# The 64 steps of a decoder's mixer phase: the same work dealt anew over five kinds of body

## What is computed

```python
x = x + mamba(layernorm(x))
x = x + cross_attention(layernorm(x), ctx, mask)       # one head of 256, softmax over 1601
x = x + routed_ffn(layernorm(x))                       # top 2 of 8 experts, width 704

def mamba(x):                                          # 512 inner channels, 16 states
    xs, res = split(x @ W_in.T)
    xs = silu(causal_conv4(xs) + b_conv)
    B = (xs @ W_x.T)[:, :16]
    dt = softplus(xs @ W_dt.T + b_dt)
    # per channel c and state n, along the tokens t:
    h[t] = exp(dt[t] * A[c, n]) * h[t - 1] + dt[t] * B[t, n] * xs[t]
    y[t] = sum_n h[t] + D[c] * xs[t]
    return (y * silu(res)) @ W_out.T
```

## Time and profile before

| what | us |
|---|---|
| median of 3 runs | 1064.59 (1064.29 to 1067.52) |
| profiled execution, span | 1119.2 |
| FIRST, from its first scan to that of the next body | 116.10 |
| STEADY, first of two | 155.30 |
| LAST | 145.00 |
| DRAIN, up to 720 us | 93.80 |

### The profile page before, as it was taken

One profiled execution on the slowest core, in us unless ns is written; L12 is line 12 of the kernel. 1 busy time (PEld: TensorE's weight loads), 2 busy tenths in 40 slices (PEclk: granted clock), 3 DMA queues, 4 the chain that ended last, 5 costly groups with the idle time before them and its releaser, 6 DMA issues. The chain is left out here.

```text
span 1119.2 us, 16281 instructions
## 1 busy us (share of the span) xinstructions
PE 908.4 (81%) x5148; PEld 723.8 (65%) x5149; DVE 670.0 (60%) x1091; ACT 446.0 (40%) x827; POOL 599.3 (54%) x499
## 2 busy tenths in 40 slices
PE   5767667899969999788998779736279999999665
PEld 2344345576856677665677647735279999999564
DVE  5188789887789877876878433275034444443215
...
GB/s 321 157 199 1 2 113 38 1 15 1 40 264 1 16 1 2 199 103 7 9 1 110 42 7 8 20 155 191 146 39 115 115 115 75 78 37 70 61 89 90
DMA packets 48955, 85.45 MB, mean 76 GB/s; under 512 B 6292, under 2 KB 38696, under 8 KB 46856
## 3 DMA queue, kind: packets, MB, share of 16 engines
...
## 5 line engine op out<-in xcount | busy, mean ns | idle before, releaser
L413 POOL TENSOR_TENSOR u<-dtx,b_all 128x512 f32<-128x512 f32 x256 | 324.9, 1281 | 176.6 <-DVE h L662 172.9
L662 DVE TENSOR_TENSOR_SCAN h<-da,u 128x512 f32<-128x512 f32 x256 | 307.5, 1215 | 55.8 <-ACT da L497 33.9
L497 ACT ACTIVATE da<-dt_,a_neg 128x512 f32<-128x512 f32 x256 | 174.5, 690 | 105.9 <-DVE h L662 105.2
L785 PEld LDWEIGHTS ysum<-ident,h 128*128 128x128 f32 x1024 | 128.4, 152 | 94.5 <-DVE h L662 45.0
L785 PE MATMUL ysum<-ident,h 128*128 128x128 f32 x1024 | 157.7, 293 | 32.5 <-DVE h L662 25.5
L1421 DVE TENSOR_TENSOR hid<-act_,ps_u 128x352 f32<-128x352 f32 x78 | 40.4, 521 | 134.7 <-ACT act_ L1272 128.4
L965 PE MATMUL pv<-pT,ctx_n 128*128 128x128 f32 (+1 forms) x832 | 104.6, 276 | 1.4 <-DVE x_all L722 1.3
L965 PEld LDWEIGHTS pv<-pT,ctx_n 128*128 128x128 f32 (+1 forms) x832 | 98.4, 192 | 6.5 <-DVE x_all L722 3.2
L936 PE MATMUL pa<-ctx_t,xnT_a 128*128 128x401 f32 (+1 forms) x256 | 94.2, 502 | 3.6 <-ACT xnT_a L548 1.8
L1272 ACT ACTIVATE act_<-ps_g 128x352 f32<-128x352 f32 x78 | 36.1, 465 | 149.9 <-PE ps_u L1535 92.6
L1559 PE MATMUL ps_y<-w_hi,hidT_hi 128*128 x234 | 68.1, 291 | 19.0 <-issue 15.0
...
## 6 DMA issues: line engine op xcount, KB each, us to landing
...
```

The source lines that it names most:

```text
L413: nc.gpsimd.tensor_tensor(u[:, i % 2, :], dtx[:, j % 2, :], b_all[:, n, :], ALU.mult).then_inc(u_ok, 1)
L497: nc.scalar.activation(da[i % DS][:], dt_[:, j % 2, :], ACT.Exp, scale=a_neg[:, j, n:n + 1]).then_inc(da_ok, 1)
L662: nc.vector.tensor_tensor_scan(h[:, i % HS, :], da[i % DS][:], u[:, i % 2, :], 0.0, ALU.mult, ALU.add).then_inc(scan_ok, 1)
L785: last = nc.tensor.matmul(ysum[:, t * P:(t + 1) * P], h[:, i % HS, t * P:(t + 1) * P], ident[:], is_transpose=True, start=n == 0 and t == ...
```

## The change

All step numbers of the five tables are dealt anew. No instruction is added or removed, no tile, semaphore or line of the engines' programs changes, nor the order in which groups are added in PSUM. The order of SP's queue is the same in both, and so is every engine's order in FILL, although most of its numbers differ. The tables are four lines longer, so what was L662 is L666 in the kernel after. The diff, cut: of each table the lines that hold the numbers spoken of below.

```diff
 STEADY = {
-    "y_copy": 1, "y_turn": 2, "read_out": 3, "out_proj": (4, 4, 4, 4), "x1": (6, 7), "ln_a_stat": 7, "ln_a_root": 8,
-    "ln_a_norm": 8, "ln_a_turn": 8, "ln_a_copy": 10, "x_bias": 11, "query_const": 10, "query": (10, 10),
-    "row_const": 12, "query_copy": 12,
+    "y_copy": 1, "y_turn": 2, "read_out": 3, "out_proj": (4, 4, 4, 4), "x1": (7, 7), "ln_a_stat": 7, "ln_a_root": 7,
+    "ln_a_norm": 7, "ln_a_turn": 7, "ln_a_copy": 11, "x_bias": 20, "query_const": 10, "query": (10, 10),
+    "row_const": 11, "query_copy": 13,
...
-    "pick": ((14, 15, 16, 17), (17, 18, 19, 21), (26, 27, 28, 29), (34, 36, 38, 39)), "fill": (14, 14, 24, 35),
+    "pick": ((14, 15, 16, 17), (17, 18, 19, 21), (23, 27, 28, 29), (35, 36, 37, 38)), "fill": (15, 17, 24, 36),
...
-    "p_turn": ((20, 22, 22, 23), (29, 30, 30, 32), (38, 39, 39, 41), (46, 47, 47, 49)),
+    "p_turn": ((21, 22, 22, 23), (29, 30, 30, 31), (38, 39, 40, 40), (44, 47, 49, 51)),
...
-    "av_copy": (30, 41, 47, 54), "out": (31, 40, 47, 54), "x2": (32, 42, 47, 58), "ln_f_stat": 58, "ln_f_root": 60,
-    "ln_f_norm": 59, "ln_f_turn": 59, "ln_f_copy": 61, "router": (59, 60, 60, 60), "scores": 63, "ln_m_stat": 0,
+    "av_copy": (29, 42, 48, 56), "out": (31, 40, 48, 53), "x2": (32, 42, 49, 56), "ln_f_stat": 56, "ln_f_root": 58,
+    "ln_f_norm": 58, "ln_f_turn": 58, "ln_f_copy": 60, "router": (59, 59, 60, 60), "scores": 62, "ln_m_stat": 0,
...
-    "tap": (5, 10, 12, 14), "conv": (4, 10, 12, 14), "res_proj": ((19, 23), (24, 25), (28, 29), (30, 31)),
+    "tap": (6, 10, 13, 14), "conv": (6, 10, 12, 14), "res_proj": ((14, 16), (24, 25), (28, 28), (29, 30)),
...
 FIRST = {
     **STEADY,
-    "ln_m_norm": 0, "ln_m_turn": 0, "ln_m_copy": 2, "in_proj": ((3, 3), (6, 7), (7, 8), (8, 9)),
...
-    "dt_proj": ((50, 51, 52, 55), (3, 5, 5, 6), (13, 16, 17, 19), (32, 32, 33, 34)), "softplus": (57, 8, 23, 38),
-    "dt_add": (57, 10, 23, 38), "dtx": (60, 14, 28, 39),
+    "softplus": (57, 9, 23, 41), "dt_add": (57, 10, 23, 41), "dtx": (59, 14, 25, 43),
 }
 LAST = {
     **STEADY,
-    "out_proj": (4, 4, 5, 5), "x1": (5, 7), "ln_a_root": 7, "query_const": 9,
+    "read_out": 2, "x1": (5, 7), "ln_a_root": 9, "ln_a_norm": 8, "ln_a_turn": 9, "ln_a_copy": 10, "x_bias": 10,
+    "row_const": 10, "query_copy": 14,
...
-    "pick": ((13, 15, 16, 17), (17, 18, 19, 21), (26, 27, 28, 29), (34, 36, 38, 39)), "fill": (13, 14, 23, 35),
...
+    "pick": ((13, 15, 16, 17), (17, 18, 19, 21), (26, 27, 28, 29), (35, 37, 39, 40)), "fill": (12, 17, 24, 34),
...
+    "av_copy": (30, 41, 47, 55), "out": (30, 39, 47, 52), "x2": (31, 41, 47, 55), "ln_f_root": 57, "ln_f_norm": 57,
```

More of the change, by code:

```diff
@@ L85 @@
+    "tap": (6, 10, 13, 14), "conv": (6, 10, 12, 14), "res_proj": ((14, 16), (24, 25), (28, 28), (29, 30)),
+    "res_copy": (27, 27, 29, 34), "silu": 35, "b_proj": (34, 34, 39, 39), "b_copy": 43,
+    "dt_proj": ((48, 54, 55, 57), (4, 4, 6, 6), (14, 19, 21, 21), (33, 34, 34, 35)), "softplus": (60, 8, 24, 37),
+    "dt_add": (60, 9, 26, 39), "dtx": (62, 14, 28, 44),
 }
@@ L87 @@
     **STEADY,
[L88 to L91 removed]
+    "ln_m_stat": 4, "ln_m_norm": 11, "ln_m_turn": 2, "ln_m_copy": 2, "in_proj": ((2, 2), (7, 8), (9, 13), (13, 16)),
+    "tap": (2, 3, 5, 7), "conv": (12, 12, 16, 17), "res_proj": ((18, 20), (20, 21), (24, 25), (26, 26)),
+    "res_copy": (7, 7, 9, 12), "silu": 17, "b_proj": (31, 31, 31, 34), "b_copy": 18,
+    "dt_proj": ((35, 35, 38, 41), (), (), ()), "softplus": (24, 7, 10, 11), "dt_add": (28, 11, 23, 27),
+    "dtx": (30, 7, 20, 24), "a_exp": 18,
 }
@@ L114 @@
     **STEADY,
-    "out_proj": (3, 3, 4, 4), "ln_a_root": 6, "ln_a_norm": 7, "ln_a_turn": 9, "query_const": 9, "row_const": 13,
-    "query_copy": 11, "score": ((12, 13, 13, 14), (15, 15, 16, 17), (22, 22, 23, 26), (31, 32, 32, 34)),
-    "pick": ((13, 14, 15, 16), (16, 17, 18, 20), (24, 25, 26, 27), (32, 34, 36, 37)), "fill": (13, 13, 25, 34),
-    "max": (16, 20, 28, 42), "exp": (18, 25, 33, 45), "inverse": (21, 24, 34, 44),
-    "p_turn": ((20, 20, 21, 21), (27, 28, 28, 30), (37, 38, 40, 40), (45, 46, 48, 49)),
-    "p_copy": ((19, 20, 21, 23), (28, 29, 30, 32), (39, 41, 42, 43), (46, 47, 48, 49)),
-    "av": ((20, 20, 20, 22, 22, 23, 27), (30, 30, 30, 33, 33, 36, 37), (40, 40, 40, 41, 41, 42, 45), (48, 48, 49, 50, 51, 51, 52)),
-    "av_copy": (29, 39, 46, 52), "out": (30, 40, 46, 55), "x2": (32, 42, 46, 56), "ln_f_norm": 63, "ln_f_turn": 56,
-    "router": (57, 59, 60, 60),
+    "read_out": 0, "out_proj": (5, 5, 5, 8), "x1": (2, 4), "ln_a_stat": 6, "ln_a_root": 12, "ln_a_norm": 12,
+    "ln_a_turn": 9, "ln_a_copy": 16, "x_bias": 15, "row_const": 13, "query_copy": 18,
+    "score": ((14, 14, 14, 15), (16, 17, 17, 18), (21, 23, 23, 24), (30, 32, 33, 34)),
+    "pick": ((13, 14, 15, 16), (16, 17, 18, 19), (21, 23, 24, 28), (32, 33, 36, 38)), "fill": (2, 10, 32, 35),
+    "max": (17, 20, 30, 40), "exp": (18, 28, 35, 44), "inverse": (21, 21, 31, 52),
+    "p_turn": ((19, 19, 20, 21), (28, 28, 29, 30), (37, 37, 40, 40), (41, 46, 47, 49)),
+    "p_copy": ((22, 23, 27, 29), (32, 33, 34, 35), (42, 44, 46, 48), (49, 51, 54, 56)),
+    "av": ((20, 20, 22, 23, 23, 23, 27), (29, 29, 29, 31, 32, 35, 37), (40, 40, 40, 40, 42, 42, 44), (46, 46, 46, 48, 48, 49, 49)),
+    "av_copy": (32, 38, 48, 57), "out": (29, 38, 46, 54), "x2": (29, 45, 46, 53), "ln_f_stat": 53, "ln_f_root": 59,
+    "ln_f_norm": 60, "ln_f_turn": 54, "ln_f_copy": 63, "router": (54, 55, 60, 63), "scores": 60,
 }
```

37 lines of the change are left out of this document (16 added, 21 removed).

## The result

The kernel after takes **1033.88 us** (median of 4 runs, 1030.95 to 1035.07) beside 1064.44 (1063.35 to 1067.52) for the kernel before: a ratio of 0.9704, with a 95% interval of 0.9685 to 0.9722, or 30.6 us less. The forecast was 1049, with a range down to 1037: the direction was right and the gain nearly twice what was said.

The account below looks back on a forecast made before the run. Bounds differ by body: GpSimd's pace in FIRST, TensorE in STEADY and DRAIN, mixed in LAST. Terms -3.0 - 5.0 - 5.0 - 2.5 - 0.5 = -16.0, carried to the timed 1064.6 as 15.2 to 16: 1049 us, range 1037 to 1065.

Parts of the forecast that it names:

- The pause of step 23: STEADY: VectorE picks row tile 2 before its fill is done, waiting about 2.9 us; costed at nothing.
- The term of 1.2 at scan 40: FIRST: a scan's wait behind a dtx product goes as dtx falls into VectorE's pause; 1.2 of 3.7 us saved.
- (a) to (c): STEADY: earlier attention LayerNorm, later first convolution, query copy and fills moved; VectorE 2.4 us earlier, nothing counted on PE.
- the two new blocks: STEADY: out-projection 3 may wait for attT, row tile 3's first turn for its exponential; +1.4 us for both.
- The gap that I priced at -2.4: STEADY: PE's 4.85 us wait before the final LayerNorm's turn shrinks to about 2.4, by earlier statistics and normalisation.
- the seam: LAST into DRAIN: earlier final LayerNorm lets PE's queue drain about two scans sooner; -2.5 us, PE's gap near 4.
- (a) read_out: LAST: last read_out from step 3 to 2, so out_proj can begin earlier; -1.5 us.
- (b) the root: LAST: attention's root on ScalarE moves behind da(8), step 7 to 9, removing the scan's 1.09 us wait; -1.1 us.
- (c) the query copy: LAST: copy from step 12 to 14, two more scans run during the 4.62 us wait; half counted, -1.2 us.
- (d) read_out 1 ahead of the pick: LAST: read_out 1 precedes row tile 3's first pick, inside VectorE's 5.03 us wait; -1.2 us.
- rival 2: Whole kernel: the whole gain comes through, VectorE's gains are kept; -26, so 1039 us; chance 0.13.
- Rival 3: STEADY and LAST: PE stands before work whose ScalarE and GpSimd steps are later; slower, +5, so 1070 us; chance 0.10.

Follow-up runs that it names:

- the tail alone: Kernel before, in STEADY only: row tile 3's last pieces, final LayerNorm, router, scores at the new steps, ratio 0.9996; at the seam, similarly in LAST only, 0.9989.
- the input work alone: Kernel before, in STEADY only: the next batch's input work and the dt groups at the steps of after; 1081.14 us, ratio 1.0141.

## Why the prediction was wrong

**What held.** TensorE's gaps are what a body's table can win: the first STEADY body got shorter by 7.5 us and its gaps by 7.1. The gap before the final turn went from 4.9 to 2.3 (forecast 2.4). FILL did nothing. The 55 us between the profiled and the timed kernel before lie in the expert phase, so carrying the sum over to the timed median nearly unchanged was right. DRAIN's table did nothing (forecast -0.5, measured -0.2 alone). The pause of step 23 is there and costs nothing: TensorE waits for nothing between the two LayerNorms. It is 1.74 us, not 2.9:

```profile
237.10 0.62 DVE L649 COPY_PREDICATED sim<-mask,pa 128x401 f32<-128x401 uint8 x1 [1.74 <-POOL mask L443]
```

**FIRST** (forecast -3.0, measured -1.3 to -1.6). The wait for u behind a product of dt and xs is gone: VectorE's longest wait for u in the body is 0.3 us, and the scans gain about 1.0 us near 28, some 0.5 near 40 and 1.2 near 61. The term of 1.2 at scan 40 was mis-sized. The wait there named ScalarE, and I had put it down to the product. The first sixteen steps cost 0.8, about the 0.7 that stood for the LayerNorm.

**STEADY** (forecast -2.5 a body, measured -6.5 to -6.8 alone). Two steps failed. The first is "nothing for (a) to (c), since the matmuls behind them were queued already", with a tenth of the gap of 1.5: all the small gaps closed (1.5, 1.4, 0.8, 0.7, 0.5 and smaller, 5.2 us), where I had counted 1.5. The second is the +1.4 for the two new blocks: in the kernel after no wait of TensorE for attT or the exponential of row tile 3 is in the trace. The danger was real, though: with the tail alone TensorE waits 2.07 us at the turns of row tile 3, for copies of turned probabilities and not for the exponential. The sum of my own terms without these two errors is -2.4 - 5.2 = -7.6, against 7.5 in the first body's profile. That it fits so well is partly luck: the second body won 5.5, with 1.4 us more ahead of its first LayerNorm.

But a sum over pieces is itself a doubtful instrument here. The gap that I priced at -2.4 closed and gave 0 when the tail alone was moved; the input work alone lost 7.8 us. Terms that are read from a gap hold only if the time saved is not waited for elsewhere, and the trace of before doesn't show where that will be. The estimate of "under 0.6 us" for the collision of VectorE and GpSimd counts the one in FIRST alone; the one gained in STEADY (1.1 a body) went with (a) at 0.

**LAST and the seam** (forecast -5.0 and -2.5; measured -13.3 and -3.9). The terms were:

- (a) read_out -1.5: alone, with two out-projections a step earlier, -2.3 in LAST; undone in the new table 0.
- (b) the root -1.1: **0**. I priced the idle time of a scan, though the scan is not what others waited for.
- (c) the query copy -1.2: **0** when undone in the new table. "Two more scans run in that time" is the step that failed: the fill, moved up to step 12, holds the u of scan 13 for as long (the wait is 2.71 us there). The copy was not moved alone in the kernel before.
- (d) read_out 1 ahead of the pick -1.2: not tried alone.
- The dt groups had **no term at all**: 7.6 us in the finished table, of which 3.7 by one softplus four steps earlier. They stood in the table and I passed over them. This is the largest failed step.
- The clock: 3.4 us, likewise without a term. It can't be added to the 7.6: with the dt groups back the turn, the constants and the query products take some 4.4 us longer than in the kernel after, and that is inside the 7.6. What makes up the rest of the 13.3 is in no run.
- The seam -2.5: -3.3 by the tail alone and -3.9 by the whole table. Mechanism right, a little small: TensorE's gap fell from 6.59 to 1.6, where I had said 4.

**The rivals.** The result went past rival 2 (1039), whose mechanism, the whole gain coming through, is what happened, but at other places: its figures were -5 a STEADY body (-6.6), -8 for LAST (-13.3) and -4 at the seam (-3.9). I gave it 0.13 because TensorE was busy for 140 of 155 us; but the gaps were the 15 us on top, and nearly all the small ones could be closed. Rival 3's blocks did not form in STEADY of the kernel after. In its LAST TensorE waits 1.7 us for copies of turned probabilities and 0.9 for attT, and in the tail run 2.07, so the mechanism exists. The range was cut just below rival 2, with no room for its own error.
